# Source dots of the attention layers: from row sums on VectorE to a turn and a product on TensorE

## What is computed

```
h = x @ W
s = h @ a_src                      # a scalar per node, read at each edge's source
d = h @ a_dst
e = s[src] + d[dst]                # each node has a self loop besides its edges
e = where(e > 0, e, 0.2 * e)
w = exp(e - segment_max(e)[dst])
alpha = w / (segment_sum(w)[dst] + 1e-16)
out = segment_sum(alpha[:, None] * h[src], dst) + b
x = x + sigmoid(out)               # three such layers
```

## Time and profile before

| | us |
|---|---|
| median of 3 runs | 6525.8 (6522.5 to 6534.7) |
| the profiled execution | 6529.2 |
| its span, first to last instruction | 6527.7 |
| PE busy | 4932.6 (76%) |
| DVE busy | 4483.4 (69%) |
| POOL busy | 4296.6 (66%) |
| ACT busy | 3646.1 (56%) |

### The profile page before, as it was taken

The page is one execution under the profiler, slowest core; times in us unless marked ns, Lnnn a source line. Parts: engine busy times, 40 slices in busy tenths (PEclk is TensorE's granted clock), DMA queues, the critical chain, the costliest instruction groups (busy, mean ns, idle before and its releaser), DMA issues. The chain is left out here.

```text
span 6527.7 us, 110704 instructions
## 1 busy us (share of the span) xinstructions
PE 4932.6 (76%) x23310; PEld 3004.7 (46%) x23310; DVE 4483.4 (69%) x12803; ACT 3646.1 (56%) x7987; POOL 4296.6 (66%) x4317
## 2 busy tenths in 40 slices
PE   4999999999984557847783666059989997776665
PEld 2665555655651134424442444036656664333332
DVE  6887877877865868858885899866655554444443
ACT  4998888988875736645662444753333332333332
POOL 4777777777730077737755775047767775777777
PEclk9999999999998968877886555579999998999998
DMA  6888878777754556646663777877767774444442
GB/s 197 269 277 270 267 261 279 249 223 224 227 185 162 189 149 199 200 126 188 203 203 121 227 231 233 258 212 223 222 202 237 235 234 147 131 129 129 126 124 91
DMA packets 889075, 1314.93 MB, mean 201 GB/s; under 512 B 294247, under 2 KB 347208, under 8 KB 882092
## 3 DMA queue, kind: packets, MB, share of 16 engines
q1 hardware_dynamic: 745906, 1077.42, 49.7%
q0 software_dynamic: 142688, 232.29, 15.1%
HBM read 660.03 MB, written 654.88 MB: 201 GB/s over the span
## 5 line engine op out<-in xcount | busy, mean ns | idle before, releaser
L1304 POOL DMA_INDIRECT g_xs<-table,g_gi x1176 | 1240.1, 1055 | 919.8 <-DMA g_gi<-in_src_lookups_dram 399.4
L1632 POOL DMA_INDIRECT n_xs<-table,n_gi x1176 | 1204.3, 1024 | 727.7 <-DMA n_gi<-lookups 358.2
L1775 DVE TENSOR_TENSOR_SCAN n_dT<-n_km,n_dT,bank 128x512 f32<-128x512 uint8 x291 | 372.4, 1280 | 1007.6 <-PE bank L1660 997.0
L1735 ACT ACTIVATE n_eT<-bank,edge_b 128x512 f32<-128x512 f32 x294 | 202.1, 688 | 803.0 <-PE bank L1677 797.2
L698 PE MATMUL bank<-n_zT,wn 128*128 128x512 f32 (+1 forms) x1176 | 542.7, 597 | 82.9 <-ACT n_sg L756 59.8
L679 PE MATMUL bank<-n_xT,gat_w 128*128 128x512 f32 (+1 forms) x1176 | 561.9, 615 | 54.0 <-issue 34.9
L1643 POOL DMA_INDIRECT out_dram<-n_xn,n_eo x392 | 432.3, 1103 | 124.8 <-issue 113.3
L619 POOL DMA_INDIRECT node_map<-p_es x392 | 401.1, 1023 | 119.5 <-issue 116.5
L647 POOL DMA_INDIRECT p_lk<-node_map,p_gi x392 | 391.3, 998 | 128.2 <-issue 106.1
L1179 DVE CUSTOM_DVE_ANT_0 g_junk<-g_xs,v_src 128x128 f32<-128x128 f32 x1176 | 272.9, 284 | 294.7 <-DMA g_xs<-table,g_gi 293.9
L614 POOL DMA_INDIRECT p_rows<-in_x_dram,p_es x392 | 393.0, 1003 | 124.8 <-issue 113.3
(11 more groups left out here) (253 smaller groups left out, 12292.2 us busy)
## 6 DMA issues: line engine op xcount, KB each, us to landing
table<-n_ro SPq DMA_DIRECT2D x768, 256.0 KB
g_gb<-decays SPq DMA_DIRECT2D x294, 256.0 KB, 4.1
n_xd<-table SPq DMA_DIRECT2D x294, 256.0 KB
table<-g_xn SPq DMA_DIRECT2D x196, 256.0 KB
g_xo<-table SPq DMA_DIRECT2D x196, 256.0 KB
edge_feats<-n_eT SPq DMA_DIRECT2D x196, 256.0 KB, 2.8
table<-n_xn SPq DMA_DIRECT2D x196, 256.0 KB
n_ea<-edge_feats SPq DMA_DIRECT2D x196, 256.0 KB
```

What stands on the lines that cost most here:

```text
L1304: q.indirect_dma_start(out=xs[g % XR][:, u, :], out_offset=None, in_=tables[l], in_offset=bass.IndirectOffsetOnAxis(ap=gi[g % 6][:, 0, u:u ...
L1632: q.indirect_dma_start(out=xs[g][:, u, :], out_offset=None, in_=tables[L], in_offset=bass.IndirectOffsetOnAxis(ap=gi[g][:, u, slot_word:sl ...
L1775: V.tensor_tensor_scan(in_order(dT[g][:, :]), kept(g), in_order(flat_banks[1]), 0.0 if begins(g) else carry(dT[g.before(1)]), ALU.mult, AL ...
```

## The change

The setup keeps the vector `W @ a_src` of each layer as one column in a zeroed buffer `v_pad` of 55 columns a layer, instead of as 128 equal rows. In `gat_pass` the gathered rows of a group are turned by four transposes into bank 4 (`turn_source`, lag 5), copied by ACT to `xT` (`copy_source`, lag 5) and multiplied, a tile at a time, with a 28-column window of `v_pad` in which only the column of that tile's place in the segment isn't zero (`source_dots`, now on PE, lag 5). The 28 products of a segment add up in `banks[7]`, which holds the dots in the softmax's layout. DVE's `source_dots`, its buffers `zz` and `junk`, and PE's `dots_to_rows` are gone. The weights' columns move to bank 6. Bank 4 is now used by both `turn_source` and `turn_back`. In the first two layers `dot`, `copy_back`, `copy_dots` and `store_dots` come one step earlier (24, 23, 25, 26).

```diff
-        v_src = sb("v_src", [P, LAYERS, C])
+        v_pad = sb("v_pad", [C, LAYERS, 2 * SG * U - 1])
...
+                    do(V.memset(v_pad[:, :, :], 0.0))
...
-                    do(V.tensor_copy(v_src[:, :, :], banks[0][:, 0:LAYERS, :]))
+                    do(V.tensor_copy(v_pad[:, :, SG * U - 1:SG * U], banks[1][:, 0:LAYERS, 1:2]))
...
-                    for l in range(LAYERS):
-                        T.matmul(banks[0][:, l, :], lhsT=att[:, l:l + 1].broadcast_to([C, P]), rhs=wT[:, l, :],
-                                 start=True, stop=True)
...
-                junk = of_ring(f"g{l}_junk", 2, c=c2)
+                xT = of_ring(f"g{l}_xT", 2, (C, U * P), c=c2)
                 ST = SG * U
-                zz = of_ring(f"g{l}_zz", 2, (P, ST), c=c2)
...
-                            v.wait_ge(pb, 6 * s + 1)
+                            v.wait_ge(sdot, SG * (s + 1))
                             landed(v, sl, s, 48)
-                            step(V.tensor_tensor(t0[k][:, :], banks[6][0:ST, 0, :], sc[k][:, 0, :], ALU.add))
+                            step(V.tensor_tensor(t0[k][:, :], banks[7][0:ST, 0, :], sc[k][:, 0, :], ALU.add))
+                            marks["dots_read", s] = n_seg[0]
...
-                        def source_dots(g):
-                            landed(v, gx, g, 16 * U)
-                            ready(v, pb, 6 * (g // SG - 2) + 1)
-                            ready(v, sdot, g - 1)
-                            for u in range(U):
-                                i = g % SG * U + u
-                                last = V.tensor_tensor_reduce(out=junk[g % 2][:, u, :], in0=xs[g % XR][:, u, :], in1=v_src[:, l, :],
-                                                              scale=1.0, scalar=0.0, op0=ALU.mult, op1=ALU.add,
-                                                              accum_out=zz[g // SG % 2][:, i:i + 1])
-                            last.then_inc(sdot, 1)
...
-                                else [(23, store_rows), (27, store_dots)]))
+                                else [(23, store_rows), (26, store_dots)]))
...
-                        def dots_to_rows(g):
...
+                        def turn_source(g):
+                            landed(pe, gx, g, 16 * U)
+                            ready(pe, raw_c, g)
+                            if not last_layer:
+                                ready(pe, copied, g - 18)
+                            for u in range(U):
+                                last = T.transpose(banks[4][:, u, :], xs[g % XR][:, u, :], ident[:, :])
+                            last.then_inc(raw_t, 1)
+
+                        def source_dots(g):
                             s = g // SG
+                            pe.wait_ge(raw_c, g + 1)
+                            if g % SG == 0 and s:
+                                pe.wait_ge(vb, marks["dots_read", s - 1])
+                            for u in range(U):
+                                i = g % SG * U + u
+                                last = T.matmul(banks[7][0:ST, 0, :], lhsT=v_pad[:, l, ST - 1 - i:2 * ST - 1 - i],
+                                                rhs=xT[g % 2][:, u * P:(u + 1) * P], start=i == 0, stop=i == ST - 1,
+                                                skip_group_check=True)
+                            last.then_inc(sdot, 1)
...
                         def turn_back(g):
                             pe.wait_ge(new, g + 1)
                             ready(pe, copied, g)
+                            pe.wait_ge(raw_c, min(g + 19, GE))
...
-                        flat(GE, [(6, max_to_row), (8, sums_to_column), (18, turn), (20, multiply)]
-                             + [(5, dots_to_rows), (6, max_to_column), (7, sums_to_row), (8, to_columns)]
-                             + ([] if last_layer else [(23, turn_back), (25, dot)]))
+                        flat(GE, [(6, max_to_row), (8, sums_to_column), (5, turn_source), (18, turn), (20, multiply)]
+                             + [(5, source_dots), (6, max_to_column), (7, sums_to_row), (8, to_columns)]
+                             + ([] if last_layer else [(23, turn_back), (24, dot)]))
...
+                        def copy_source(g):
+                            a.wait_ge(raw_t, g + 1)
+                            ready(a, sdot, g - 1)
+                            S.activation(xT[g % 2][:, :], flat_banks[4], ACT.Copy).then_inc(raw_c, 1)
...
-                        flat(GE, [(7, weights), (16, scale), (20, add_half), (21, gate)]
-                             + ([] if last_layer else [(24, copy_back), (26, copy_dots)]))
+                        flat(GE, [(5, copy_source), (7, weights), (16, scale), (20, add_half), (21, gate)]
+                             + ([] if last_layer else [(23, copy_back), (25, copy_dots)]))
```

More of the change, by code:

```diff
@@ L990, in gat_pass @@
             vb, pb, ab = (sem(f"g{l}_{k}") for k in ("softmax_step", "softmax_turned", "softmax_weights"))
-            sdot, scaled, selfed, turned, summed, product, tanh, half, new, final, back, copied, dotted, dots_out = (
-                sem(f"g{l}_{k}") for k in ("source_dots", "scaled", "self_added", "turned", "summed", "product", "tanh", "half",
+            raw_t, raw_c, sdot, scaled, selfed, turned, summed, product, tanh, half, new, final, back, copied, dotted, dots_out = (
+                sem(f"g{l}_{k}") for k in ("src_turned", "src_copied", "source_dots", "scaled", "self_added", "turned", "summed", "product", "tanh", "half",
                                            "new_rows", "final_rows", "turned_back", "copied", "dotted", "dots_copied"))
@@ L1094, in max_carry @@
                             s = g // SG
-                            v.wait_ge(pb, 6 * s + 2)
+                            v.wait_ge(pb, 5 * s + 1)
                             if s == 0:
@@ L1106, in arguments @@
                             s, k = g // SG, g // SG % 2
-                            v.wait_ge(pb, 6 * s + 3)
+                            v.wait_ge(pb, 5 * s + 2)
                             ready(v, ab, s - 1)
@@ L1134, in sum_carry @@
                             s, k = g // SG, g // SG % 2
-                            v.wait_ge(pb, 6 * s + 4)
+                            v.wait_ge(pb, 5 * s + 3)
                             step(V.tensor_copy(pc[k][:, :], banks[6][0:1, 3, 64:64 + ST]))
@@ L1145, in shares @@
                             s, k = g // SG, g // SG % 2
-                            v.wait_ge(pb, 6 * s + 5)
+                            v.wait_ge(pb, 5 * s + 4)
                             ready(v, decay_st, 16 * (s - 1))
@@ L1166, in columns @@
                             s, k = g // SG, g // SG % 2
-                            v.wait_ge(pb, 6 * s + 6)
+                            v.wait_ge(pb, 5 * s + 5)
                             ready(v, scaled, SG * (s - 1))
                             ready(v, selfed, SG * (s - 1))
-                            step(V.tensor_copy(cols[k][:, :, :], banks[7][:, 0:2, 0:ST]))
+                            step(V.tensor_copy(cols[k][:, :, :], banks[6][:, 0, 0:64].rearrange("p (k t) -> p k t", k=2)[:, :, 0:ST]))
                             marks["columns", s] = n_seg[0]
-                        def source_dots(g):
-                            landed(v, gx, g, 16 * U)
-                            ready(v, pb, 6 * (g // SG - 2) + 1)
-                            ready(v, sdot, g - 1)
-                            for u in range(U):
-                                i = g % SG * U + u
-                                last = V.tensor_tensor_reduce(out=junk[g % 2][:, u, :], in0=xs[g % XR][:, u, :], in1=v_src[:, l, :],
-                                                              scale=1.0, scalar=0.0, op0=ALU.mult, op1=ALU.add,
-                                                              accum_out=zz[g // SG % 2][:, i:i + 1])
-                            last.then_inc(sdot, 1)
                         def add_self(g):
@@ L1218, in final_rows @@
                              .then_inc(final, 1)
-                        flat(GE, [(6, logits), (7, arguments), (8, sum_carry), (9, columns), (5, source_dots), (17, add_self),
+                        flat(GE, [(6, logits), (7, arguments), (8, sum_carry), (9, columns), (17, add_self),
                                   (6, max_carry), (7, sums), (8, shares), (19, sum_edges), (22, new_rows)]
@@ L1317, in _ @@
                         pe.wait_ge(pre_v, marks["own"])
-                        def dots_to_rows(g):
-                            if g not in ends:
-                                return
-                            s = g // SG
[L1323 to L1326, removed]
+                        def turn_source(g):
[7 more added lines that the diff above has]
+                        def source_dots(g):
+                            s = g // SG
+                            pe.wait_ge(raw_c, g + 1)
[7 more added lines that the diff above has]
+                            last.then_inc(sdot, 1)
```

(4 more changed lines are left out.)

2 lines of the change are left out of this document (1 added, 1 removed).

## The result

The changed kernel takes 6721.7 us (median of 5 runs, 6711.7 to 6727.5) against 6525.7: a ratio of 1.030, 95% interval 1.0286 to 1.0314. The forecast was 6492, range 6468 to 6556. The profiled execution has a span of 6725.9 us, 198.2 more than the one of before. One of e4's ten executions took 9308 us at a granted clock of 0.57, a slower state of the chip; it is left out of the time given for e4.

The account below looks back on a forecast made before the run. POOL's gather pace plus a drain of about 80 us was taken to bound each pass. Shorter gathers -36, PE's lag in the drains +4, lower lags -2: -34 us, so 6492 us on the median, range 6468 to 6556.

Parts of the forecast that it names:

- new waits: PE waits for a gather's landing, as DVE did before at the same lag: no price.
- Put on ACT: One 587 ns copy more: ACT 3.86 us a group, bank 4 loop 3.9 and some 0.3, below POOL's 5.24: nothing.
- The slack: Some eight groups free in the ring of 20 gather buffers, hiding PE's lag at a pass's start from POOL.
- PE's own work and clock: PE's step 5.03 to 5.42 us, taken as 5.1, under POOL's 5.24; a hardly stopping PE keeps 2.4 GHz.
- the first rival: PE becomes the bound in the first two passes at 5.6 us a step: 6551 us, chance 0.22.
- a third pass at 1.2 GHz: Rival: the third pass's clock stays at 0.50, PE's step 6.3 to 7.1 us: 6586 us, chance 0.06.
- the softmax waits: PE's waits on DVE's softmax in the first two passes, up to 0.39 us a step, taken as covered in a longer step.
- The gain from POOL: Gathers 28, 28 and 35 ns shorter in the three passes once DVE drops the source dots: 36 us less.
- The bounds: POOL's gain: 25 us below, from early stretches; 45 us above, from the dots' share of DVE's two-operand time.
- The contrary reading: A two-SBUF-input VectorE instruction disturbs only GpSimd instructions reading SBUF, so POOL's gain would be 0.
- The end of a pass: Lags of the dot, its copy and store one lower: about 1 us less in each of the first two passes.

Follow-up runs that it names:

- e4: e1 with the copy of the turned source rows (copy_source) moved from ACT to DVE, ahead of add_self: 6525.9 us (nine runs), ratio to before 1.0014.
- e1: The changed kernel with the dots' copy (copy_dots) ahead of the turned rows' copy (copy_back) on ACT: 6523.9 us, ratio to before 1.0011.
- e8: The changed kernel with even and odd groups' dots in different partitions of bank 5, ACT's order unchanged: 6518.5 us, ratio to before 1.0004.
- e2: The kernel before with dot, both copies and the dots' store one step earlier, source dots still on DVE: 6569.0 us, ratio to before 1.0068.
- e3: The kernel before with its source dots left out, DVE clearing their columns instead: 6495.0 us, ratio to before 0.9964.
- e5: e1 with the third pass's addition of the raw rows replaced by writing one column, their load kept: 6491.8 us, one run.
- e7: e1 with tanh written back to PSUM, new_rows first on DVE, and the third pass's new rows kept in PSUM: 6448.4 us, again 6441.1.

## Why the prediction was wrong

**The step that failed** is that of the new waits, with the loop priced under "Put on ACT". That text followed one ring through bank 4 (source turn, ACT's round, turn back's copy) and found 3.9 us. It took the lags of dot and copies, one lower, as a microsecond won at the end of a pass, and put the new waits at nothing. It never asked what the dot waits for in its own step. The ring that decides goes through bank 5: turn back, its copy, the dots' copy, the dot, next step. Its length is PE's work of a step plus 1.24 us, 6.27 to 6.60 and 6.37 at the mean, against POOL's 5.36. Both ends of each wait could be read from the lags and the two lists: the dot of lag 24 waits for the copy of lag 25 of the group before, so in the same step; that copy is last in ACT's list, behind one that with lag 23 waits for PE's lag 23. e1, e8 and e2 show it.

**The slack was too large as well.** The text gave POOL eight free groups by the ring of 20 gather buffers. In the changed kernel's three passes POOL waited 4.4 us in all for a buffer; it waited for its indices. SP's loads stand in one order with its stores, and SP waited for the dots in the late stretch (2560:2820, the waits view of SP's queue):

```profile
SPq L1276 <- ACT g_dt L1444: 113.4, 41, 4.2
```

The index load for group s comes behind the dots' store of group s-27. Indices, not buffers, limited POOL's lead. This decides only when POOL begins to wait, not how large the step is: PE's steps are those of the ring from the second dot of a pass.

**PE's own work and clock were right.** The sum was 5.03 and the choice 5.1; a plain step without its gap took 5.03 and the mean of seven 5.13. That the sum fits to the hundredth is partly luck: the source turn took 0.49 instead of 0.56 (2705.31 to 2705.80) and the turn 0.53 instead of 0.59, the turn back 0.66 instead of 0.53. The granted clock of the first pass was 1.00 in 2400:2780, and 0.77 over the third. So the first rival, PE as the bound by its work or clock, did not happen, nor did a third pass at 1.2 GHz. The slower time came from a ring that no rival named. The rival with PE as the bound had the right side of the time, by luck: its causes, the softmax waits and the clock, were not the ones.

**The gain from POOL was half right.** The forecast took 36 us from the gathers' length, between 25 and 45. e3 shows 23 (13 to 33), e1 nothing. So with the ring opened the kernel would still have missed the forecast, by some 30 us (6524 against 6492). The bounds took the dots' share of DVE's two-operand time, as if each microsecond of it cost the same. e5 and e7 show that the two long ones, L1210 and L1217 of 650 to 690 ns, weigh more than the dots' 283 ns. The contrary reading, that a two-operand instruction of DVE doesn't disturb descriptor making, stood beside the forecast from the Trainium skill, SBUF — State Buffer, Who interferes with whom. The runs speak against it for these gathers: with one operand moved to PSUM they fall from 1148 ns (e1) to 978 (e7). They do not refute the page's rule that such an instruction contends with a GpSimd instruction that reads SBUF: an indirect gather has its indices there, and no run tells whether it is that read which is held up.

**The end of a pass** did not get 1 us shorter in the changed kernel: by e2 the lower lags cost 26 us a drain. With the ring open, in e1, the drains are 77.9 and 79.1 us against 82.2 and 82.7 before, so there the sign was right.

Left open: what sets the moment at which DVE's long operations meet a gather, by which e4 gains 52 ns in two passes and loses in the third. That this moment decides is read from the traces of e1 and e4; no edit tried it by itself. That the ring is the cause of the 196 us is shown by e1, e8 and e2, which leave no rival.

## What to carry to other kernels

When a lag or a bank is changed in hand-ordered queues, follow every wait round until it comes back to its own engine, and add up the work between: a wait for the same step, behind an instruction that waits for the same step of the first engine, puts both engines in series. A lag that is hidden in the steady state still shows in the drain of each pass. And where one engine only issues gathers, look at what lengthens its instruction before shifting work between the others.

## What the runs showed of the hardware

- DVE operations on 128x512 with both operands in SBUF lengthen an indirect gather of POOL: with the addition of the third pass left out, 1148 to 1067 ns; with one operand of both long operations in PSUM, 978, near the median of 944. DMA traffic of a quarter MB a group did not matter (1143).
- It depends on the moment. In e1's 2400:2780, the 24 gathers in which `new_rows` began after the first 400 ns took 940 to 947 ns; the 55 in which it already ran, or began in the first 200 ns, took 1284 at the mean.
- The operations themselves pay little for the PSUM operand: the last addition takes 692 ns in e7, by its line, against 675.

```profile
L1205 DVE TENSOR_TENSOR g_xm<-bank,g_xr 128x512 f32<-128x512 f32 x66 | 45.6, 692 | 2.3
```
